# Load order of the first stage, the places of routing steps and the last stores of an adaLN and mixture-of-experts kernel

## What is computed

```python
# conditional LoRA, rank 16, 8 factors mixed by cond_8
out  = einsum('btc,oc->bto', x, W_base) + b_base
h    = einsum('btc,erc->bter', x, As)
x1   = out + einsum('bter,eor,be->bto', h, Bs, w) * 2
# router: softmax over 8 experts, top 2, weights normalised and times 2.5
# routed experts (F = 352): (silu(t @ w_gate) * (t @ w_up)) @ w_down
# shared expert (F = 704) over all tokens, same form
return x + routed + shared
```

## Time and profile before

| | us |
|---|---|
| median of the runs | 510.59 |
| lowest and highest run | 508.84, 510.64 |
| profiled execution, whole | 506.99 |
| its span (first to last instruction) | 505.3 |

### The profile page before, as it was taken

How to read it: one execution, slowest core, us unless ns; L and a number is a source line. 1 busy time by engine, 2 the same in 40 slices (tenths; PEclk the granted TensorE clock), 3 DMA queues, 4 the chain that set the end, 5 groups by cost and what they waited for, 6 DMA issues and landing times.

```text
span 505.3 us, 10018 instructions
## 1 busy us (share of the span) xinstructions
PE 490.5 (97%) x3071; PEld 448.2 (89%) x3072; DVE 355.4 (70%) x765; ACT 261.1 (52%) x525; POOL 249.9 (49%) x367
## 2 busy tenths in 40 slices
PE   8999999999999999989999999999999899999996
PEld 7998988888888889988889999999998899888886
DVE  3666778898987556766676677676675666479896
ACT  3567785556663445565455555545554444444322
POOL 2042246655551454666967767677667674211100
PEclk9999999999999999999999999999999999999999
DMA  8387569156222234534344444444444442599942
GB/s 225 130 281 224 169 186 310 57 179 201 45 83 43 84 93 126 119 103 125 104 114 116 114 116 123 123 117 117 112 114 116 115 105 68 145 370 322 384 140 83
DMA packets 104938, 74.54 MB, mean 148 GB/s; under 512 B 61946, under 2 KB 99844, under 8 KB 104900
## 3 DMA queue, kind: packets, MB, share of 16 engines
q1 hardware_dynamic: 95780, 55.21, 37.1%
q0 software_dynamic: 6816, 18.62, 12.5%
q10 hardware_dynamic: 2304, 0.26, 0.5%
HBM read 40.25 MB, written 20.32 MB: 120 GB/s over the span
## 4 chain that ended last, share of the span: by engine, by line
PE 75%; DVE 15%; ACT 5%; issue 4%; DMA 1%; another core or an unknown queue 0%; DVEq 0%; ACTq 0%
PE bank L274 17%; PE bank L276 17%; PE bank L275 17%; PE bank L790 9%; PE bank L762 5%; PE bank L792 5%; DVE bank L1222 2%; ACT gt_h L952 1%; DVE acc L1333 1%; DVE xt_l L1034 1%; ACT x_half L872 1%; DVE x L1058 1%; DVE pos L1081 1%; DMA xin<-in_x_dram 1%; PE bank L576 1%
## 5 line engine op out<-in xcount | busy, mean ns | idle before, releaser
L274 PE MATMUL bank<-w_all,rt_h 128*128 x284 | 97.6, 344 | 0.0
L276 PE MATMUL bank<-w_all,rt_l 128*128 x284 | 91.6, 323 | 0.0
L275 PE MATMUL bank<-w_all,rt_h 128*128 x284 | 91.5, 322 | 0.0
L790 PE MATMUL bank<-w_all,gt_h 128*128 (+1 forms) x213 | 78.0, 396 | 0.2 <-issue 0.2
L551 POOL DMA_INDIRECT y_rows<-y_sb,dst_i x71 | 72.5, 1021 | 11.2 <-POOL spare L465 10.4
L544 POOL DMA_INDIRECT rows<-x_halves,tok_i x71 | 69.5, 978 | 12.5 <-issue 2.2
L952 ACT CAST gt_h<-bank 128x512 fp32r<-128x512 f32 (+1 forms) x48 | 28.1, 586 | 88.7 <-DVE bank L1222 79.8
L274 PE MATMUL bank<-xs_h,sg_h 128*128 128x512 f32 x176 | 70.6, 401 | 0.3 <-DVE gt_h L1233 0.3
L275 PE MATMUL bank<-xs_l,sg_h 128*128 128x512 f32 x176 | 68.9, 391 | 0.0
L276 PE MATMUL bank<-xs_h,sg_l 128*128 128x512 f32 x176 | 68.7, 390 | 0.0
L1295 DVE TENSOR_TENSOR g<-bank,act 128x352 f32<-128x352 f32 x71 | 37.2, 524 | 41.7 <-issue 24.5
(11 more groups left out here) (180 smaller groups left out, 1155.6 us busy)
## 6 DMA issues: line engine op xcount, KB each, us to landing
pick<-y_rows SPq DMA_DIRECT2D x16, 512.0 KB, 7.8
xin<-in_x_dram SPq DMA_DIRECT2D x8, 512.0 KB, 4.8
x_halves<-x_half SPq DMA_DIRECT2D x8, 512.0 KB, 3.3
w_own<-in_L_ffn_w_gate_dram SPq DMA_DIRECT2D x8, 352.0 KB, 4.5
w_own<-in_L_ffn_w_up_dram SPq DMA_DIRECT2D x8, 352.0 KB, 4.7
y_sb<-in_x_dram SPq DMA_DIRECT2D x5, 512.0 KB, 3.5
base_rows<-y_sb SPq DMA_DIRECT2D x5, 512.0 KB, 2.8
acc<-base_rows SPq DMA_DIRECT2D x5, 512.0 KB, 7.1
```

Source lines behind the costliest of these rows:

```text
L274: pe.matmul(o, lh, rh, start=start, stop=False, skip_group_check=skip)
L275: pe.matmul(o, lh, rl, start=False, stop=False, skip_group_check=skip)
L276: return pe.matmul(o, ll, rh, start=False, stop=stop, skip_group_check=skip)
L790: pe.matmul(YE[par][:, 0:2 * D].rearrange("p (h d) -> p h d", h=2), gt_h[par][0:n, cols], both, start=(c == 0), stop=False, skip_group_che ...
```

## The change

It does the following.

- At the start SP issues `base_raw` first, then the first rows in two parts of 256 KB with a semaphore each, then `cond_in`. `g_raw` and `b_row` move to ScalarE's queue, between `a_raw` and `b_raw`. TensorE turns the base weights ahead of the first rows, turns the first rows by halves, folds by halves between them, and turns the condition last. ScalarE and VectorE take the parts in the matching order, and `main(0, 0)` waits for each half of `wa_l` by itself.
- `rank()` moves from behind unit 5 to behind the gate product of unit 6, ahead of `down(4)`.
- `hot_tiles` gives 2 tiles instead of 3 to units with `c = 4`. So the tiles per unit from unit 9 are 3, 2, 1, 1, 3, 3, 3, 2, 1, 1, 3, 3, 3, 2, 1 in place of 3, 3, 1, 1, 3, 3, 3, 3, 1, 1, 3, 3, 3, 1; the last is tile 31 in unit 23 and not 22, and `LIST_AT` is 24 and not 23.
- The budget of steps ahead of `g_low(8)` is 2 instead of 3.
- The last unit's low part is made in two halves of 256 columns, and the last `down` waits for the second half ahead of its third tile.
- The store of tile 2 of the last group goes to ScalarE's queue.

```diff
-            first.append(min(first[-1] + (1, 3, 3, 3, 3, 1)[w % NC], NT))
+            first.append(min(first[-1] + (1, 3, 3, 3, 2, 1)[w % NC], NT))
 # SP, start
-            load_x(0)
             sp.dma_start(base_raw[:], w_base.rearrange("(k p) c -> p k c", p=P)).then_inc(s_dw, 16)
-            sp.dma_start(g_raw[:], gate_w).then_inc(s_dg, 16)
-            sp.dma_start(b_row[:], b_base.rearrange("(k p) -> k p", p=P)).then_inc(s_dc, 16)
+            for first, here in ((0, s_x_two), (2, s_xin[0])):
+                sp.dma_start(xin[0][:, first:first + 2, :],
+                             x_rows[first * P:(first + 2) * P, :].rearrange("(t p) d -> p t d", p=P)).then_inc(here, 16)
+            sp.dma_start(cond_in[:], cond).then_inc(s_dcond, 16)
 # SP, end
-            for n, (first, end) in enumerate(((0, 2), (2, 3), (3, 4))):
+            for n, (first, end) in ((0, (0, 2)), (2, (3, 4))):
 # TensorE, main
+                    if i == 0 and t == 0:
+                        pe.wait_ge(s_wal, k + 1)
 # TensorE, start (the base weights' turn stands here now, then g_raw and b_row, then:)
+            pe.wait_ge(s_x_two, 16)
+            for k in range(K):
+                turn_two(k, 0)
+            pe.wait_ge(s_gate, 1)
+            fold(0)
+            pe.wait_ge(s_xin[0], 16)
+            for k in range(K):
+                turn_two(k, 2).then_inc(s_tx, 1)
+            fold(1)
+            pe.wait_ge(s_cond, 1)
+            pe.wait_ge(s_atl, 1)
+            pe.transpose(bank[7][:, K * P:K * P + NB], cond_er[:], ident[0:NB, 0:NB]).then_inc(s_cT, 1)
             lora_in(0)
-            pe.wait_ge(s_wal, K)
 # TensorE, down
+                    if (j, c, t) == (NG - 1, NC - 1, 2):
+                        pe.wait_ge(s_gl, u + 2)
 # TensorE, units
                 gate(j, c)
+                if u == RANK_AT + 1:
+                    rank()
                 if u >= 2:
                     down(*order[u - 2])
                 for t in hot_tiles(u - 2):
                     permute(t)
                 up(j, c)
-                if u == RANK_AT:
-                    rank()
 # ScalarE, start and end
-            sc.dma_start(cond_in[:], cond).then_inc(s_dcond, 16)
+            sc.dma_start(g_raw[:], gate_w).then_inc(s_dg, 16)
+            sc.dma_start(b_row[:], b_base.rearrange("(k p) -> k p", p=P)).then_inc(s_dc, 16)
...
-            x_high(0)
             sc.wait_ge(s_gT, 1)
             sc.copy(gate_t[:], bank[6][:, 0:K * (E + 1)]).then_inc(s_gate, 1)
+            base_high(0)
+            x_high(0)
+            base_high(1)
             sc.wait_ge(s_cT, 1)
             sc.copy(w_er[:], bank[7][:, K * P:K * P + NB]).then_inc(s_wer, 1)
...
+            sc.wait_ge(s_fin, 2 * (NG - 1) + 2)
+            sc.dma_start(out_rows[T - 2 * P:T - P, :], acc[NG - 1][:, 2, :]).then_inc(s_out, 16)
 # VectorE
+            base_low(0)
             x_low(0, 0)
             x_low(0, 1)
+            base_low(1)
...
+                    for h in range(2):
+                        cols = slice(h * 2 * P, (h + 1) * 2 * P)
+                        v.tensor_tensor(gt_h[p][HALF:P, cols], G_B[p][0:HALF, cols], gt_h[p][0:HALF, cols].bitcast(F32),
+                                        ALU.subtract).then_inc(s_gl, 1)
...
-            steps_at = {0: (0, 8), ..., 8: (3, 1000)}
+            steps_at = {0: (0, 8), ..., 8: (2, 1000)}
```

More of the change, by code:

```diff
@@ L613, in _ @@
             mm.then_inc(s_aT, 1)
-            turn_x(0)
+            pe.wait_ge(s_dw, 16)
+            for k in range(K):
+                for o in range(K):
+                    pe.transpose(bank[2 + k][:, o * P:(o + 1) * P], base_raw[:, o, k * P:(k + 1) * P], ident[:])
             pe.wait_ge(s_dg, 16)
@@ L619, in _, with turn_two, fold @@
             pe.transpose(bank[6][:, K * E:K * (E + 1)], b_row[:], ident[0:K, 0:K]).then_inc(s_gT, 1)
-            pe.wait_ge(s_cond, 1)
-            pe.wait_ge(s_atl, 1)
-            pe.transpose(bank[7][:, K * P:K * P + NB], cond_er[:], ident[0:NB, 0:NB]).then_inc(s_cT, 1)
-            pe.wait_ge(s_dw, 16)
-            for k in range(K):
-                for o in range(K):
-                    pe.transpose(bank[2 + k][:, o * P:(o + 1) * P], base_raw[:, o, k * P:(k + 1) * P], ident[:])
-            pe.wait_ge(s_gate, 1)
-            for k in range(K):
+            def turn_two(k, first):
+                for t in (first, first + 1):
+                    mm = pe.transpose(TX[k][:, t * P:(t + 1) * P], xin[0][:, t, k * P:(k + 1) * P], ident[:])
+                return mm
+            def fold(k):
                 for o in range(K):
@@ L1058, in add_bias, with base_low @@
                 v.tensor_tensor(x1[i % 2][:, t, :], MAIN[t][:, 0:DX], bias[:], ALU.add).then_inc(s_x1, 1)
-            x_low(0, 0)
-            x_low(0, 1)
-            for k in range(K):
+            def base_low(k):
                 v.wait_ge(s_wah, k + 1)
```

20 lines of the change are left out of this document (12 added, 8 removed).

## The result

The kernel after takes 511.81 us (median of 20 runs, 507.07 to 516.84) against 508.86 for the kernel before on the same chip (20 runs, 503.51 to 514.48). The ratio is 1.0059 with an interval from 1.0031 to 1.0087, so about 3.0 us slower. The forecast of no change was wrong.

A forecast was written before the change was run, and what follows sets the result against it. TensorE, busy 97% of the span, was taken as the bound. Terms -0.2 + 0 - 0.6 + 1.1 - 0.35 summed to -0.05 us, so a median of 510.5 us (same, 0.84), range 508.4 to 512.1.

The forecast's parts named there:

- The start: Reordered first loads up to the turn of `b_raw`: 0.2 us gained, between 0.5 gained and 0.5 lost.
- The rank product: Moved ahead of `down(4)`: its 0.59 us wait goes but returns at `down(4)`, so 0, at most 0.75 us gained.
- The named next-late step: Unit 4's low part, right behind which `down(4)` starts; TensorE would arrive at 86.7 us and wait for it.
- Units 8 to 13: Smaller budget at unit 8 and one tile less in unit 10: 0.6 us gained.
- The term for down(8): `g_low(8)` no longer behind `blk_cmp`, ends 0.48 us sooner; `down(8)` starts at 104.1 us.
- The list a unit later: Token list in unit 24 delays the last expert's weights and first gather: 1.1 us lost, bounds 0 and 1.6.
- Rival A: The late list costs nothing, as the gather or turning DMA has slack: 509.4 us, chance 0.22.
- B: Second routed block's rows also late by 1.2 us, and the start loses 0.2: 512.1 us, chance 0.13.
- The end: Halved last low part and third store on ScalarE's queue: 0.35 us gained, between 0.28 and 0.6.

The follow-up runs named there:

- e6: After, with the store and reload of `y_sb` on SP's queue put ahead of the wait for `blk_e` and the experts' weights; ratio 1.0033.
- e9: Before with the change's rank product place, end and budget 2, the SP order of e6, and 2 one-hot tiles at `c = 4` and `c = 5`; ratio 0.9995.
- e10: As e9, but with the change's start, `b_raw` issued right behind `a_raw`, and `g_raw` and `b_row` on SP; ratio 0.9990.
- e11: After with `b_raw` issued right behind `a_raw`, and `g_raw` and `b_row` on SP; 502.68 us in its one run beside 500.85 of before.
- e12: Before with the change's start alone; ratio 1.0043.
- e13: Before with 2 one-hot tiles at `c = 4` alone, so the list a unit later; median 516.25 us of 6 beside 511.26, no ratio.
- e14: Before with the budget of 2 steps ahead of `g_low(8)` alone; ratio 1.0041.
- e1: After with the budget ahead of `g_low(8)` put back to 3; ratio 1.0040.
- e5: After with the sum that the `blk_e` clip reads placed in PSUM and not SBUF; ran only once, no ratio.
- e4: After with the `blk_e` clip as a `tensor_tensor` with a constant instead of a `tensor_scalar`; ran only once, no ratio.
- e7: After with the start of before on all engines; ratio 1.0029.
- e8: Before with the two routing settings alone: budget 2 ahead of `g_low(8)` and 2 one-hot tiles at `c = 4`; ratio 1.0031.
- e3: After with both the budget of 3 and the old one-hot tile numbers put back; ratio 0.9997.
- e2: After with the old one-hot tile numbers put back, so the list is made in unit 23; ratio 0.9982.

## Why the prediction was wrong

**The start: predicted -0.2, about +0.7 on the mean of the traces.** The 0.7 is the difference of the two means above, from eight and seven single executions of which the eight lie between 11.12 and 13.70, so it is an estimate whose size is not shown. After's own profile has -0.27 and looks like a hit; that was luck of the one execution. But the size of the term was taken from one landing, "it is there only at 11.2, just ahead of its use". The bounds (0.5 gained to 0.5 lost) were worked out from the issue's shift alone, not from how much such a landing scatters. An arrival of TensorE at 11.1, 0.1 us ahead of a load that takes 8.7 us in runs of 64 bytes, had no slack. In four of the eight executions with the new start TensorE waits 0.42, 0.94, 1.78 and 1.85 us for it. To these 0.7 come the stretches at half clock behind such waits (1.56 us in e6).

**The rank product: predicted 0, measured 0.** The wait reappears as 0.77 us at `down(4)`, which starts at +0.01. The named next-late step was the right one. But the 0 is not general. The last routing step ahead of `mul(4)`, at 84.81 in the earlier trace rows, takes 0.70 us there because GpSimd holds it. In e9, e10 and e11 it takes 0.18, and with the moved product `down(4)` comes 0.51, 0.38 and 0.99 sooner (in e11 another step, `prob`, takes 0.42 and not 1.48 too). In e12, e13 and e14 it takes 0.18 as well, but the old place of the product keeps the gain to 0.04 to 0.13.

**Units 8 to 13: predicted -0.6, measured -0.46 at down(8), and 0 at down(11).** The term for down(8) is right. What failed is the way from there to down(11), "TensorE ... would arrive at 114.85 and goes on". I followed `blk_cmp` behind `g_low(8)` as a step of a fixed 0.75 us and said nothing of the two steps behind it. The last of them moved under a GpSimd instruction, took 1.10 us and not 0.19, and delayed `mul(9)` to 106.30 from 105.79. `down(10)`, which was to come 0.24 sooner, comes 0.52 later, and the lighter unit 10 only makes that good. Where it doesn't happen (e1, e5, e13), the 0.6 to 0.75 at down(11) are there as predicted.

**The missed step: the reload of `y_sb`, 0 predicted, +1.85 in after, 0.8 to 1.7 in e4, e7, e8, e11 and e14.** This is the step that failed most. The prediction put it at nothing without a reason: nothing in it asks who waits for `blk_e`. SP does, with eight issues of about 0.5 us, a store and the reload behind it on the same queue. The 1.0 us by which its first issue moves (105.43 to 106.40) become 1.7 at the reload's issue (115.75 to 117.41), since the store takes 7.0 us and not 6.4 from its issue. TensorE waits at down(12) for the sums that wait for the reload. In before that sum already waited 0.62 us for the load, a row that the prediction left out, as it went by the waits of TensorE alone. That row would also have told that a gain at down(11) can't be kept.

**The list a unit later: predicted +1.1, measured +1.2.** From down(24) to the first block, the nine kernels with the late list lose 1.2 to 1.6 (mean 1.4), the seven others 0.1 to 0.2. The chain is the one named: `mul(25)` at 172.71 behind the list, the weights at 173.92, the gather at 180.41 (in before 177.40), and waits of 0.76 and 0.49 on TensorE. Rival A, a free list, is refuted by e13, and B by the second wait, which is 0.49 and not 1.2.

**The end: predicted -0.35, measured -0.27.** The low part's 0.28 is all that comes through. The second store is now issued on ScalarE's queue 0.33 us behind the first, and the last one on SP 0.66 behind the first (503.20), as soon as its sum is done, and not 0.93. Yet the last store lands 2.76 us behind the first issue in after and 2.75 in before, so the second queue gave nothing. From the last product that reads `xs` to the end of the span it is 8.05 to 8.08 us in the traces with the new end and 8.32 to 8.35 in those with the old.

**The sum.** 0.7 for the start, 1.3 for the reload (the mean of the jumps in after, e4, e7 and e8, 1.85, 1.70, 0.78 and 0.96), 0 for the rank product and the units, 1.2 for the list and -0.27 for the end make 2.9; 3.0 were measured. This is an estimate: the first two terms scatter by 0.5 us and more between executions, so the close fit is in part luck, and what the stage of the blocks adds or takes is not in it. The forecast's -0.05 had the list and the end nearly right, the rank product right for this execution and the start with the wrong sign, it kept a gain of 0.6 in units 8 to 13 that is lost again, and it lacked the reload. That the stated range holds 511.81 is luck too. The range was built on a median of 510.59 for before, which took 508.86 in the comparison; the measured ratio on 510.59 gives 513.6, above the range. The chance of 0.08 for slower counted on two of the named rivals together, and the reload was not among them.

## What to carry to other kernels

When a step is moved by one place, list everyone who waits for its last instruction, queues included, and read the waits of the engines that feed the bottleneck, not only its own. A load that lands "just ahead of its use" in one trace is a scatter, not a number: ask for more slack than its landing varies. A VectorE step on SBUF operands can last until the GpSimd instruction that it meets has ended, so look at what GpSimd does at the step's new place, or let the step read PSUM.

## What the runs showed of the hardware

- A VectorE step of 0.19 us with its operands in SBUF takes 1.10 us when it starts while a GpSimd instruction runs, and ends 0.05 us behind it (after); with the input in PSUM it takes 0.22 (e5). A reduction over SBUF values (`top_v`, 0.42 us) is not held in before.
- When the two start within a few ns it can go either way: `top_w` takes 0.70 us in before and 0.18 in e9, both 4 to 6 ns behind GpSimd's start.
- Behind an idle time of TensorE of 0.86 to 1.85 us in the start the granted clock went to its half level for about 3 us in two of the traces (e1, e6). Behind waits of 0.42, 0.94 and 1.78 (e3, e2, e5) it stayed at 1.00 in the rows, so the length of the wait alone doesn't decide it.
- The second 64 KB part of `b_raw`, in runs of 64 bytes, took 7.9 to 10.7 us from issue to landing where it shared the DMA engines with the first rows, and at most 4.4 and 5.7 when issued ahead of them.
